# filter_edges: softplus behind its group's first eviction, message rows in four buffers, source row as int16 in memory

## What is computed

```python
h = x @ w_in + b_in
Wij = ssp(f_ij @ w_f1 + b_f1) @ w_f2 + b_f2          # ssp(v) = softplus(v) - log 2
Wij = Wij * rcut_ij[:, None]
x_ij = h[idx_j] * Wij
agg = jax.ops.segment_sum(x_ij, idx_i, num_segments=n_atoms)
```

## Time and profile before

| | us |
|---|---|
| median of 3 runs | 8095.7 |
| lowest and highest run | 8090.58, 8124.99 |
| the profiled execution's own time | 8101.87 |
| its span in the profile | 8100.6 |
| first eviction (L757) of the first group, start | 528.0 |
| first eviction of the last group, start | 1961.8 |

### The profile page before, as it was taken

The page is one execution under the profiler, slowest core; times in us unless marked ns, Lnnn a source line. Parts: engine busy times, 40 slices in busy tenths (PEclk is TensorE's granted clock), DMA queues, the critical chain, the costliest instruction groups (busy, mean ns, idle before and its releaser), DMA issues. The chain is left out here.

```text
span 8100.6 us, 109148 instructions
## 1 busy us (share of the span) xinstructions
PE 4629.1 (57%) x24927; PEld 3727.6 (46%) x24928; DVE 3777.2 (47%) x9811; ACT 1475.1 (18%) x3554; POOL 3622.3 (45%) x3791
## 2 busy tenths in 40 slices
PE   6646666666982333324566677677067735554556
PEld 4535555554752222223444445455056635444546
DVE  7636666665933333335333333333466643333333
ACT  6424445543011000001111111111000010000001
POOL 0045566665103666662354544444033325555552
PEclk9757777777975555556777777677566655555556
DMA  2046666664411111111455555556533311111111
GB/s 61 7 138 184 182 189 190 191 189 133 102 38 42 45 45 45 45 45 32 131 154 150 156 147 154 149 153 146 55 110 101 97 53 44 43 45 43 44 43 36
DMA packets 888536, 801.63 MB, mean 99 GB/s; under 512 B 324630, under 2 KB 754424, under 8 KB 888360
## 3 DMA queue, kind: packets, MB, share of 16 engines
q1 hardware_dynamic: 740984, 483.21, 22.8%
q0 software_dynamic: 138544, 314.22, 13.4%
q10 hardware_dynamic: 8960, 3.68, 0.2%
HBM read 621.39 MB, written 179.34 MB: 99 GB/s over the span
## 5 line engine op out<-in xcount | busy, mean ns | idle before, releaser
L1183 POOL DMA_INDIRECT sum_rows<-table,sum_idx x1664 | 1576.4, 947 | 1349.2 <-ACT sum_idx L1198 684.9
L1465 POOL DMA_INDIRECT edges_kv<-kv,edges_idx x896 | 851.4, 950 | 1065.0 <-issue 565.6
L911 POOL DMA_INDIRECT by_src<-edges_rows,edges_pos x832 | 885.8, 1065 | 579.8 <-issue 360.9
L1259 DVE TENSOR_TENSOR a_acc<-a_acc,sum_p_sum 128x128 f32 x1664 | 476.2, 286 | 1227.3 <-remote 955.6
L1295 PE MATMUL sum_p_sum<-sum_hot,sum_rows 128*128 128x128 f32 x1664 | 384.1, 411 | 838.7 <-DVE a_acc L1259 635.2
L1558 DVE TENSOR_TENSOR edges_kv<-edges_kv,edges_p_e 128x512 f32<-128x512 f32 x448 | 298.1, 684 | 1077.2 <-remote 563.5
L1295 PE MATMUL sum_p_sum<-sum_hot,sum_msg 128*128 128x128 f32 x1664 | 398.1, 426 | 678.5 <-ACT sum_msg L1205 583.9
L1607 PE MATMUL edges_p_e<-k_wekv,edges_attrT 128*128 128x256 f32 x1792 | 645.2, 516 | 185.9 <-issue 184.1
L1295 PEld LDWEIGHTS sum_p_sum<-sum_hot,sum_rows 128*128 128x128 f32 x1664 | 338.6, 302 | 884.4 <-DVE a_acc L1259 701.7
L1295 PEld LDWEIGHTS sum_p_sum<-sum_hot,sum_msg 128*128 128x128 f32 x1664 | 358.0, 322 | 714.9 <-issue 714.9
L1607 PEld LDWEIGHTS edges_p_e<-k_wekv,edges_attrT 128*128 128x128 f32 x1792 | 437.1, 260 | 310.6 <-issue 233.0
(11 more groups left out here) (354 smaller groups left out, 8665.3 us busy)
## 6 DMA issues: line engine op xcount, KB each, us to landing
edges_attr<-by_src SPq DMA_DIRECT2D x112, 512.0 KB
v<-edges_kv SPq DMA_DIRECT2D x112, 512.0 KB, 3.6
sum_vv<-v SPq DMA_DIRECT2D x112, 512.0 KB, 3.9
edges_src_b<-in_src_row SPq DMA_DIRECT2D x104, 512.0 KB
edges_attr<-in_attr128T SPq DMA_DIRECT2D x104, 512.0 KB
edges_near<-h_in SPq DMA_DIRECT2D x832, 48.0 KB
sum_rows<-by_src SPq DMA_DIRECT2D x112, 264.0 KB, 2.9
edges_src_b<-rel SPq DMA_DIRECT2D x112, 256.0 KB
```

The lines of the kernel that those rows point to most:

```text
L911: nc.gpsimd.indirect_dma_start(Dr.by_src0, bass.IndirectOffsetOnAxis(pos[:, h, j:j + 1], 0), rows[:, h, j, :], None).then_inc(scattered[h] ...
L1183: nc.gpsimd.indirect_dma_start(rows[:, q, j, :], None, Dr.table, bass.IndirectOffsetOnAxis(idx[:, q, j:j + 1], 0)).then_inc(fetched[q], 16)
L1259: nc.vector.tensor_tensor(out=window, in0=window, in1=p_sum[:, j // 4, j % 4, :], op=ALU.add).then_inc(added, 1)
L1465: nc.gpsimd.indirect_dma_start(kv[:, q, j, :], None, Dr.kv, bass.IndirectOffsetOnAxis(idx[:, q, j:j + 1], 0)).then_inc(fetched[q], 16)
```

## The change

Three things change in `filter_edges`, and one small stage before it.

1. **Softplus moves on ACT and DVE.** ACT did the four softplus steps of group g+1 at the end of group g, ahead of the first eviction of g+1. Now it does the steps of g right behind the first eviction of g. On DVE the last step moves ahead of `neighbours`, and its result `sp` has one buffer instead of two.
2. **`rows` has four buffers** and four semaphores instead of two. `sums` now waits for the second eviction of its own group before it writes the ends. `positions` still waits for the scatters of group g-2. `loT` has one buffer.
3. **The source row is int16**, read from the scratch tensor `src16`. The old `rows_from_first` becomes `rows_of_ends`, which also makes `src16`: a cast on DVE, seven transposes on PE, seven copies on ACT, seven stores on SP, these ahead of the stores of the target row.

The core of the diff:

```diff
-    src_b = s.sb("src_b", [P, L, GE], I32)
+    src_b = s.sb("src_b", [P, L, GE], I16)
...
-    sp = s.sb("softplus", [P, 2, GE // 2])
+    sp = s.sb("softplus", [P, GE // 2])
...
-    rows = s.sb("rows", [P, 2, G, XR])
+    rows = s.sb("rows", [P, L, G, XR])
...
-                nc.sync.dma_start(src_b[:, q, :], A["src_row"][:, edges].broadcast_to([P, GE])).then_inc(landed[q], 16)
+                nc.sync.dma_start(src_b[:, q, :], Dr.src16[:, edges].broadcast_to([P, GE])).then_inc(landed[q], 16)
...
-            def group(g, h, last, uses):
-
+            def group(g, q, last, uses):
+
+                h = q % 2
                 act.wait_ge(hd_ready, g + 3)
                 nc.scalar.copy(hd[:, h], p_hd[:]).then_inc(hd_kept, 1)
+                softplus(g, h)
                 act.wait_ge(attr_ps, g + 3)
                 if uses is not None:
-                    act.wait_ge(scattered[h], uses * 16 * G)
+                    act.wait_ge(scattered[q], uses * 16 * G)
                     act.sem_inc(tick, 1)
-                nc.scalar.copy(rows[:, h, :, 0:XM], p_hd[:]).then_inc(attr_kept, 1)
+                nc.scalar.copy(rows[:, q, :, 0:XM], p_hd[:]).then_inc(attr_kept, 1)
...
                 ins.then_inc(ws_ready, 1)
-                if not last:
-                    softplus(g + 1, 1 - h)
...
-                dve.wait_ge(w_ready, 2 * g + 2)
-                nc.vector.tensor_add(sp[:, h, :], re[:], ln[:]).then_inc(sp_ready, 1)
+                dve.wait_ge(w_ready, 2 * g + 4)
+                nc.vector.tensor_add(sp[:], re[:], ln[:]).then_inc(sp_ready, 1)
...
                 if uses is not None:
-                    dve.wait_ge(scattered[h], uses * 16 * G)
+                    dve.wait_ge(scattered[(q + 2) % L], uses * 16 * G)
...
+                dve.wait_ge(attr_kept, g + 2)
+                dve.sem_inc(tick, 1)
+                nc.vector.tensor_copy(rows[:, q, :, XS:XR], K.ends[:, bass.ds(g * G, G), :])
...
-                    sums(g - 1, 1 - h)
-                    products(g - 1, 1 - h)
+                    sums(g - 1, (q - 1) % L)
+                    products(g - 1, (q - 1) % L)
+                softplus(g, h)
                 neighbours(g, q)
-                softplus(g, h)
                 pick(g, h, first)
```

More of the change, by code:

```diff
@@ L22 @@
 I32 = mybir.dt.int32
+I16 = mybir.dt.int16
 BF16 = mybir.dt.bfloat16
@@ L409, in _, with rows_of_ends, at @@
             nc.scalar.activation(K.root[:], K.root[:], ACT.Sqrt).then_inc(root, 1)
-def rows_from_first(nc, K, s, numbers, row16):
+def rows_of_ends(nc, K, Dr, s):
     chunks = [(c, min(P, T - c * P)) for c in range(-(-T // P))]
[L416 to L419, removed]
+    low, src = s.sb("from_first", [P, T]), s.sb("src", [P, T])
+    turned, turned_src = s.sb("turned", [P, len(chunks), P], BF16), s.sb("turned_src", [P, len(chunks), P], I16)
+    p_first, p_t, p_s = s.ps("p_first", [P, 1024]), s.ps("p_t", [P, -(-T // 512), 512]), s.ps("p_s", [P, -(-T // 512), 512])
+    first_ready, low_ready, src_ready, t_ready, s_ready, c_ready, kept, stored = (s.sem(n) for n in ("first", "low", "src", "t", "s", "c", "kept", "stored"))
+    def at(to, c, n):
+        return to[0:n, c // 4, c % 4 * P:(c % 4 + 1) * P]
     with nc.Block() as block:
@@ L432, in _ @@
                 n = min(512, T - c)
-                mm = nc.tensor.matmul(p_first[:, c:c + n], K.ones[0:1, :], numbers[0:1, c:c + n], start=True, stop=True)
+                mm = nc.tensor.matmul(p_first[:, c:c + n], K.ones[0:1, :], K.dst_f[0:1, c:c + n], start=True, stop=True)
             mm.then_inc(first_ready, 1)
+            pe.wait_ge(src_ready, 1)
+            for c, n in chunks:
+                tr = nc.tensor.transpose(at(p_s, c, n), src[:, c * P:c * P + n], K.ident[:])
+            tr.then_inc(s_ready, 1)
             pe.wait_ge(low_ready, 1)
             for c, n in chunks:
-                tr = nc.tensor.transpose(p_t[0:n, c // 4, c % 4 * P:(c % 4 + 1) * P], low[:, c * P:c * P + n], K.ident[:])
+                tr = nc.tensor.transpose(at(p_t, c, n), low[:, c * P:c * P + n], K.ident[:])
             tr.then_inc(t_ready, 1)
@@ L441, in _ @@
         def _(sp):
[L442 to L445, removed]
+            for row16, of, ready in ((Dr.src16, turned_src, kept), (Dr.dst16, turned, c_ready)):
+                for c, n in chunks:
+                    sp.wait_ge(ready, c + 1)
+                    nc.sync.dma_start(row16.rearrange("a (t p) -> (a t) p", p=P)[c * P:c * P + n, :], of[0:n, c, :]).then_inc(stored, 16)
+            sp.wait_ge(stored, 32 * len(chunks))
 def layer_norm_stats(nc, K, s):
@@ L703, in group @@
                 for j in range(G):
-                    mm = nc.tensor.matmul(p_first[:, j * NB:(j + 1) * NB], loT[:, h, j * P:(j + 1) * P], place[:, h, :, j], start=True, stop=True)
+                    mm = nc.tensor.matmul(p_first[:, j * NB:(j + 1) * NB], loT[:, j * P:(j + 1) * P], place[:, h, :, j], start=True, stop=True)
                 mm.then_inc(first_ready, 1)
@@ L901, in _ @@
                 nc.gpsimd.indirect_dma_start(Dr.by_src0, bass.IndirectOffsetOnAxis(K.pad_i[:, b:b + 1], 0), K.pad_row[:], None).then_inc(padded, 16)
-            with nc.gpsimd.Fori(0, NG // 2) as i:
-                for h in range(2):
-                    g = i * 2 + h
+            with nc.gpsimd.Fori(0, NG // L) as i:
+                for q in range(L):
+                    g, h = i * L + q, q % 2
                     pool.wait_ge(pos_ready, g + 3)
@@ L2107, in build @@
     with Space(nc, "k") as k:
-        K.soft = [k.sem(f"soft{q}") for q in range(4)]
+        K.soft, K.padded = [k.sem(f"soft{q}") for q in range(4)], k.sem("padded")
         K.x = k.sb("x", [P, NB, D])
```

64 lines of the change are left out of this document (36 added, 28 removed).

## The result

The changed kernel takes **8221.06 us** (median of 4 runs, 8211.39 to 8227.66) beside 8110.34 for the kernel before: ratio **1.0136, interval 1.0104 to 1.0168**. I had said 7844, range 7800 to 7960. The profiled execution took 8215.15, span 8213.9.

A forecast was written before the change was run, and what follows sets the result against it. A loop of waits through ACT and PE bound `filter_edges` at 13.92 us a group; POOL's 11.13 plus 0.27 remainder gives 11.40. 103 periods save 259.6, less 3.3 and 4: 252 us, so 7844 us, range 7800 to 7960.

The forecast's parts named there:

- I take it that PE's signals come late while SP is issuing loads.: In `filter_edges`, SP's load issuing was said to delay PE's signals, by up to 2.3 us for `p_w`.
- I take the lower value, 8.3, for ACT's loop rather than 10.6.: ACT's loop without the softplus steps: 8.3 us a group without late signals, 10.6 with them.
- The leg of 7.95 us: The part of ACT's loop from the start of PE's transposes to the next `w_cut`, 7.95 us.
- POOL is the nearest wall: POOL's eight scatters with gaps need 11.13 us a group, claimed as the bound after the change.
- Rival A: Scatters get longer or signals stay late by half: about 12.3 us a group, 7936 us in all; chance 28%.
- Rival B: The refill's loads hide the gather's signal from the first eviction: a 14.7 us loop, 8183 us in all; chance 8%.
- a lateness of 2.3: Argument against Rival B: the gather's signal 2.3 us late gives 4.3 + 6.4 = 10.7 us, still under POOL.
- Rival C: No change: DVE's softplus sum 2.5 us late makes `p_w` wait, 13.9 us a group, near 8100 us; chance 4%.
- worth 0 alone: Four `rows` buffers gain nothing by themselves; they let ACT run ahead.
- +3.3: Cost in us of seven more stores on SP in `rows_of_ends`, 0.47 each.
- the +4 for the start: One-time cost of 4 us before the first `products`, as group 0's softplus steps now follow the first eviction.
- The DMA share would be 0.70: The DMA engines' load in `filter_edges`, 0.64 before, would be 0.70 after and not the bound.

The follow-up runs named there:

- e10: The changed kernel, unaltered, run again where the kernel before takes 6683.05 us: 6644.47 us, ratio 0.9948.
- e2: The changed kernel with the softplus steps and the sum put back in their old places: 6667.36 us against 6681.17, ratio 0.9978.
- e13: The changed kernel with one shared `near` load a group, so SP issues 6 loads, not 13; kernel before at 8218.33 us: ratio 1.0007.
- e16: e2's kernel again, where the kernel before takes 8115.74 us: 8104.34 us, ratio 0.9988.
- e9: e2's kernel again, where the kernel before takes 6692.62 us: ratio 0.9972.
- e6: The changed kernel with `neighbours` ahead of `sums` and `products` on DVE, releasing the refill earlier: 8195.09 us against 8110.66, ratio 1.0107.
- passes A and C: Extra `filter_edges` passes put ahead of the changed kernel's real one: A without scatters, 9.38 us a group; C without scatters and with one load, 9.15.
- e17: The changed kernel with three extra `filter_edges` passes: 64 byte scatter rows, 11.06 us a group; half the scatters, 9.36; POOL clearing tiles instead, 9.52.

## Why the prediction was wrong, by its steps

- **"I take it that PE's signals come late while SP is issuing loads."** This is the step that failed. I compared a group with the start of the stage, where `near` was not yet being issued. Two things were missing there, and I named one: the scatters of pads end at 522.89 and the first scatter of rows is at 538.17, around the 528 to 534.7 that I took as the clean chain. Pass A keeps every load and drops the scatters: no lateness, 9.38 us. Pass B keeps the scatters with one load: 449 us of late signals before `w_cut`, 13.91 us.
- **"I take the lower value, 8.3, for ACT's loop rather than 10.6."** The step rests on the first. ACT's chain without lateness is short indeed: 9.4 us in pass A, softplus and all, so the 11.13 of POOL would have held. But beside the scatters, 10.83 us of them, `p_w`'s signal came no earlier when 2.49 us were taken out of ACT ahead of it. ACT only waited longer: 7.76 us idle before `w_cut` in the group shown, where it had 3.92, and 6.7 us beyond `p_w`'s records, where it had 3.05. The leg of 7.95 us in my sum was elastic.
- **"POOL is the nearest wall", 11.13 us; forecast 11.4.** Right where signals are prompt: 11.34, scatters 0.30 apart, `positions` waiting 251 us for the scatters' DMAs as written. The size of the gain was not: 38.6 us, 0.37 us a group, so the kernel before takes some 11.7 us a group there, near POOL's bound itself (worked out; it has no trace in that condition). My 252 us was counted from a period that only the lateness made. Part of the small gain is in the scatters: 1079 ns in e10 and 1101 in e2, 8 x 0.022 = 0.18 of the 0.21 us between their periods.
- **Rival A, longer scatters:** their mean fell, 1045 ns against 1065 over all 832 of each trace (1068 in the window of the earlier trace rows). Half of the lateness remaining: all of it remained, and more. My reading of the long scatters was half of the story. In the trace of before, the 90 scatters that start under the softplus sum take 1.39 us in the mean and the 71 that start under `src_lo_hot` 1.40, those two having both inputs in SBUF; the 93 under the scan, with one input in PSUM, take 0.96, as do the 325 that start under no DVE instruction. I wrote that the trace disagrees with the page of the Trainium skill (SBUF — State Buffer, Who interferes with whom). It does not: the same section says that a `tensor_tensor` with both inputs in SBUF contends with what GpSimd reads there, and these rows agree.
- **Rival B, slower:** priced at 14.7 us, measured 15.01, at a chance of 0.08. The side and the price were right, the mechanism only in part. In a regular group it is `p_w`'s signal that waits and not the gather's. The gather's does wait in 18 groups, but not until the last `near` load is out: the eviction at 1132.85 starts in the middle of a refill that ends at 1139.18, and with one `near` load (e13) the same wait is 195 us. The refill is worth 1.0 us of the period, beside the scatters. So the price was met partly by luck. My case against B, "a lateness of 2.3", again took the lateness for a constant.
- **Rival C, DVE's sum late:** no. The sum starts at 1102.90 and PE goes from its bias product at 1103.78 without a gap; `p_w` is early, its signal is not.
- **`rows`, int16, the wait in `sums`:** e16 (0.9988) and e2, e9 (0.9978, 0.9972) agree with "worth 0 alone", up to 0.3% better. `rows_of_ends` is 13.65 us long where its predecessor took 11.35: +2.3, not +3.3. The first eviction is 1.67 us later and the first `products` 4.7 (541.27 against 536.56), close to the +4 for the start.
- **A slip in the sums:** 11.8 us a group give 8095.7 - 103 x 2.12 + 7 = 7884, not 7892. Nothing hangs on it.
- **"The DMA share would be 0.70":** 0.74 and 212 GB/s in e10, between 500 and 1600; at 15 us a group, 0.55.

**Open.** Why the signal comes 11.7 us after the first scatter now and 10.3 before, which is the loss itself. With one load a group it is 9.50 (pass B) and with thirteen 11.66 in the same program, so the loads lengthen it. With six it is 11.16 or 11.74 (e13, without or with the groups at both ends), which shows no step from six to thirteen, and releasing them earlier hardly brought it back (e6, 11.57 or 10.99). Also open: whether it is a scatter's issuing or its bytes, and what makes a comparison late or prompt.

## What to carry to other kernels

A stretch that looks clean differs from the loop in everything that hasn't started yet, not only in the suspect: list all engines there before blaming one. When a wait ends in no visible cause, its length may follow another engine's burst and not the work ahead of it. Cutting work in front of such a wait bought nothing here, so such a wait should not be counted as a fixed leg of a sum. Run the kernel before again before believing a period: here over a sixth of the time (8110 against 6680) came and went with the condition, and the sign of the change with it.

## What the runs showed of the hardware

- In the late condition, while POOL issues indirect DMAs, PE's signal for `w_cut` reaches ACT 3.1 us (before) or 5.8 us (changed) after the last record in the median, 9.7 at most. Eight `near` loads on SP take up to 12.7 us in the changed kernel's trace. Without the scatters, in the same program, both are prompt: 0.24 us, and 3.93 to 3.95 us for the eight loads. ACT's and DVE's own work keeps its length: 715 and 886 us busy in pass A, 714 and 897 in the real pass.
- The granted clock was 0.86 and 0.87 of full in passes A and C, and 0.73 and 0.71 in B and the real one, where PE stands more. That is a mean over stretches at either level, 1.2 and 2.4 GHz.
- An indirect scatter of 128 rows costs POOL 1.08 us with rows of 64 and of 776 bytes alike (e17, prompt). It takes 0.96 us when no DVE instruction runs at its start, and 1.39 to 1.40 under a DVE `tensor_tensor` of 0.7 us or more with both inputs in SBUF (the trace of before).
